# RGCN sums: one gathered chunk of every 64 fetched by SP, row by row

## What is computed

```python
seg  = concatenate([edge_type * n + src, (edge_type + R) * n + dst])
srcs = concatenate([dst, src])
for l in range(2):
    agg = segment_sum(output[srcs], seg, 2 * R * n).reshape(2 * R, n, -1)
    hidden = output @ W[-1] + b[-1]
    for r in range(R):
        for inv in (0, 1):
            s = r + R * inv
            msum = agg[s] @ W[s] + count[s] * b[s]
            hidden = 2.0 * (hidden + msum) / cnt[s]
    output = relu(hidden) if l == 0 else hidden
```

## Time and profile before

| | us |
|---|---|
| median of 3 runs | 4944.46 |
| lowest and highest | 4937.94, 4947.11 |
| time of the profiled execution | 4950.41 |
| its span | 4949.1 |

### The profile page before, as it was taken

One profiled execution on the slowest core, in us unless ns is written; L12 is line 12 of the kernel. 1 busy time (PEld: TensorE's weight loads), 2 busy tenths in 40 slices (PEclk: granted clock), 3 DMA queues, 4 the chain that ended last, 5 costly groups with the idle time before them and its releaser, 6 DMA issues. The chain is left out here.

```text
span 4949.1 us, 59313 instructions
## 1 busy us (share of the span) xinstructions
PE 3702.3 (75%) x16869; PEld 2389.1 (48%) x16871; DVE 2441.6 (49%) x3834; ACT 956.0 (19%) x2715; POOL 2069.4 (42%) x2229
## 2 busy tenths in 40 slices
PE   5977957798999989999898666676668444444459
PEld 2544523365555535555455555565555433333345
DVE  7989989216888841011327543444437422222221
ACT  2946848131000041111211000000001000000011
POOL 0000013104776501011012577777763777777740
PEclk7978979899999989999999765565559655555569
DMA  0000025717888726266264311111116211111114
GB/s 18 0 0 0 0 93 213 235 50 244 295 294 291 243 102 223 90 219 223 90 222 180 132 53 53 53 53 53 52 47 246 66 53 53 53 53 53 53 63 164
DMA packets 165366, 578.54 MB, mean 117 GB/s; under 512 B 47552, under 2 KB 59425, under 8 KB 164844
## 3 DMA queue, kind: packets, MB, share of 16 engines
q0 software_dynamic: 97200, 308.78, 19.4%
q1 hardware_dynamic: 67638, 267.41, 14.9%
q10 hardware_dynamic: 390, 0.60, 0.0%
HBM read 445.10 MB, written 131.53 MB: 117 GB/s over the span
## 5 line engine op out<-in xcount | busy, mean ns | idle before, releaser
L2126 PE MATMUL ps_sum_rgcn<-gathered_rgcn,select_sum_rgcn 128*128 x3328 | 987.0, 444 | 690.6 <-DMA gathered_rgcn<-by_dst,row 371.3
L2126 PEld LDWEIGHTS ps_sum_rgcn<-gathered_rgcn,select_sum_rgcn 128*128 128x128 f32 x3328 | 770.1, 311 | 766.9 <-issue 762.6
L2041 POOL DMA_INDIRECT gathered_rgcn<-by_dst,row x782 | 740.8, 947 | 238.3 <-issue 234.7
L2041 POOL DMA_INDIRECT gathered_rgcn<-by_src,row x686 | 647.3, 944 | 246.8 <-issue 202.4
L718 PE MATMUL ps_sum_arma<-gathered_sum_arma,select_sum_arma 128*128 128x384 f32 x1664 | 552.1, 491 | 20.7 <-DMA gathered_sum_arma<-arma,other 18.2
L704 POOL DMA_INDIRECT gathered_sum_arma<-arma,other x416 | 393.4, 946 | 378.2 <-POOLq L790 209.4
L1644 PE MATMUL ps_sum_arma<-pair_counts_sum_arma,parts_sum_arma 128*128 128x448 f16 x2625 | 520.6, 354 | 5.1 <-DMA pair_counts_sum_arma<-pairs 5.1
L2195 DVE TENSOR_TENSOR select_sum_rgcn<-one_hot_sum_rgcn,ps_coef_sum_rgcn 128x2048 f32<-128x2048 bf16 x52 | 119.0, 2288 | 680.3 <-PE ps_sum_rgcn L2126 680.2
L718 PEld LDWEIGHTS ps_sum_arma<-gathered_sum_arma,select_sum_arma 128*128 128x128 f32 x1664 | 308.8, 190 | 263.8 <-issue 60.3
L752 DVE TENSOR_TENSOR acc_arma_end<-acc_arma_end,ps_sum_arma 128x768 f32 x416 | 396.9, 954 | 57.8 <-PE ps_sum_arma L718 35.5
L2159 ACT COPY sums_or_hidden_rgcn<-ps_sum_rgcn 128x128 f32<-128x128 f32 x100 | 26.6, 266 | 1869.2 <-PE ps_sum_rgcn L2126 1869.2
(11 more groups left out here) (451 smaller groups left out, 5236.2 us busy)
## 6 DMA issues: line engine op xcount, KB each, us to landing
pair_counts_sum_arma<-pairs SPq DMA_DIRECT2D x125, 800.0 KB, 4.3
by_src<-rows_rgcn_src_table SPq DMA_DIRECT2D x50, 576.0 KB, 2.8
by_dst<-rows_rgcn_dst_table SPq DMA_DIRECT2D x50, 576.0 KB, 3.7
exact<-whole_pairs SPq DMA_DIRECT2D x25, 800.0 KB
pairs<-whole_pairs POOLq DMA_DIRECT2D x25, 800.0 KB, 5.8
pair_counts_sum_x<-pairs SPq DMA_DIRECT2D x25, 800.0 KB, 4.5
pair_counts_sum_gcn<-pairs SPq DMA_DIRECT2D x25, 800.0 KB, 4.5
air_counts_sum_neighbour<-pairs SPq DMA_DIRECT2D x25, 800.0 KB, 4.4
```

The costliest lines, as they stand in the source:

```text
L2041: nc.gpsimd.indirect_dma_start(got[:, n % PLACES, :], None, table, bass.IndirectOffsetOnAxis(ap=o.row[:, n % C:n % C + 1], axis=0)).then_i ...
L2126: nc.tensor.matmul(ps[:, bass.ds(slot, P)], select[:, parity, u, :], rows[:, bass.ds(place, D)], start=False, stop=False, skip_group_check ...
```

## The change

Five edits, all for the RGCN sums:

1. SP fetches the chunk of place 63 in 12 of the 13 turns: 128 transfers of one row of 512 bytes each, whose row number SP has loaded into a register (16 at a time, from a list `by_rows` on one partition). POOL leaves these chunks out.
2. Before the fetch of turn i SP waits until item 64i + 23 is done. PE waits for all 128 rows of turn i before item 64i + 60.
3. POOL's first 16 waits go by a list, `named`: for each group of four chunks the exact number of items up to its last chunk, in place of a number that allows for 24 second uses.
4. `EARLY` is 52 in place of 48.
5. The last additions to `acc` are made in 5 pieces of 5 tiles for each order.

To prepare 1 and 3, `sum_x` writes the row numbers to DRAM (two more loads, 768 numbers of 4 bytes each), `sum_gcn` reads them back on one partition, and `ring_lists` has 33 more instructions on DVE.

```diff
-EARLY = 3 * U
+EARLY = 3 * U + GROUP
+NAMED = 16
 SHARED = NT - 1

+def by_rows(n):
+
+    return n % PLACES == PLACES - 1 and fetched(n)
...
 def ring_lists(nc, k, tile_of, place_of, then):
+
+    chunk_of = tile_of[:, 0, :]
+    for g in range(NAMED):
+        upto = float(g * GROUP + GROUP - 1)
+        then(nc.vector.tensor_scalar(chunk_of, k.orders[0].chunk_of[:, :], upto, None, ALU.is_le))
+        then(nc.vector.tensor_reduce(k.named_f[:, g:g + 1], chunk_of, AX.X, ALU.add))
+    then(nc.vector.tensor_scalar(k.named[:, :], k.named_f[:, :], float(U), None, ALU.add))
...
+        def fetch_rows(sp):
+
+            def chunk(i, table):
+
+                for p in range(0, P, U):
+                    at = nc.values_load_multi_w_load_instructions(
+                        k.by_rows[0:1, bass.ds(i * P + p, U)], engines=(mybir.EngineType.SP,), min_val=0,
+                        max_val=NP * R - 1, skip_runtime_bounds_check_because="rows of the tables")[1]
+                    for u in range(U):
+                        sp.dma_start(got[p + u:p + u + 1, PLACES - 1, :], table[bass.ds(at[u], 1), :]).then_inc(rows_landed, 16)
+
+            first_of_next = len([t for t in ROW_TURNS if t * PLACES + PLACES - 1 < C])
+            chunk(0, tables[0])
+            for start, end, table in ((1, first_of_next, tables[0]), (first_of_next, len(ROW_TURNS), tables[1])):
+                with sp.Fori(start, end) as i:
+                    sp.wait_ge(multiplied, i * PLACES + SHARED + U)
+                    chunk(i, table)
...
             for n in range(EARLY, TOTAL * U):
-                if not fetched(n):
+                if not fetched(n) or by_rows(n):
                     continue
+                if n == PLACES:
+                    named = nc.values_load_multi_w_load_instructions(
+                        k.named[0:1, 0:NAMED], engines=(mybir.EngineType.Pool,), min_val=U, max_val=C + U,
+                        skip_runtime_bounds_check_because="counts of items")[1]
                 if n % Q == 0 and n >= PLACES:
-                    gp.wait_ge(multiplied, n + Q - PLACES + SHARED + U)
+                    g = (n - PLACES) // GROUP
+                    gp.wait_ge(multiplied, named[g] if g < NAMED else n + Q - PLACES + SHARED + U)
...
                     g = (at * U + u) // GROUP
+                    if g == GROUPS - 1 and (skipped is not None or i in ROW_TURNS):
+                        pe.wait_ge(rows_landed, (i + 1) * (16 * P))
...
             for n in range(ORDERS):
-                if n:
-                    dve.wait_ge(added, n)
-                dve.wait_ge(taken, n * NT + NT)
-                nc.vector.tensor_tensor(acc[:, :, :], acc[:, :, :], sums[:, n, :, :], ALU.add).then_inc(added, 1)
+                for g in range(TURNS):
+                    here = slice(g * J, g * J + J)
+                    dve.wait_ge(taken, n * NT + g * J + J)
+                    if n:
+                        dve.wait_ge(added, g + 1)
+                    nc.vector.tensor_tensor(acc[:, here, :], acc[:, here, :], sums[:, n, here, :], ALU.add).then_inc(added, 1)
```

More of the change, by code:

```diff
@@ L1960, in fetched, with of_turn @@
     return n % C < CHUNKS
+def by_rows(n):
+    return n % PLACES == PLACES - 1 and fetched(n)
 def due(group, turn):
-    return sum(fetched(t * PLACES + group * GROUP + m) for t in range(turn + 1) for m in range(GROUP))
-def ring_lists(nc, k, tile_of, place_of, then):
+    chunks = [t * PLACES + group * GROUP + m for t in range(turn + 1) for m in range(GROUP)]
+    return sum(fetched(n) and not by_rows(n) for n in chunks)
+def of_turn(group):
+    return sum(not by_rows(group * GROUP + m) for m in range(GROUP))
+ROW_TURNS = [t for t in range(2 * C // PLACES) if by_rows(t * PLACES + PLACES - 1)]
+def ring_lists(nc, k, tile_of, place_of, then):
+    chunk_of = tile_of[:, 0, :]
[4 more added lines that the diff above has]
+    then(nc.vector.tensor_scalar(k.named[:, :], k.named_f[:, :], float(U), None, ALU.add))
     for n, o in enumerate(k.orders):
@@ L2018, in typed_sum_stage, with _ @@
         block = c.block()
[L2020 to L2024, removed]
+        (rows_landed,) = c.sems("rows_landed")
+        def fetch_rows(sp):
[12 more added lines that the diff above has]
+                    chunk(i, table)
+        @block.sync
+        def _(sp):
+            for to, source in loads:
+                sp.dma_start(to, source).then_inc(loaded, 16)
+            fetch_rows(sp)
+            if loads:
                 sp.wait_ge(loaded, 16 * len(loads))
+            sp.wait_ge(rows_landed, 16 * P * len(ROW_TURNS))
         def after(i, at, steps):
@@ L2117, in step @@
                     g = (at * U + u) // GROUP
+                    if g == GROUPS - 1 and (skipped is not None or i in ROW_TURNS):
+                        pe.wait_ge(rows_landed, (i + 1) * (16 * P))
                     if skipped is not None:
[L2119 removed]
+                        pe.wait_ge(arrived[g], ((i + 1) * of_turn(g) - skipped[g] + before[g]) * 16)
                     elif due(g, i) > due(g, i - 1):
@@ L2138, in _ @@
             for start, end in ((0, HALFWAY), (HALFWAY + 1, TURNS_OF_STEPS - 1)):
-                skipped = [start * GROUP - due(g, start - 1) for g in range(GROUPS)]
+                skipped = [start * of_turn(g) - due(g, start - 1) for g in range(GROUPS)]
                 with pe.Fori(start, end) as i:
@@ L2269, in scaled, with dram_rows @@
     return finish
+def dram_rows(k, dram, n):
+    mine = [i for i, t in enumerate(ROW_TURNS) if (t * PLACES + PLACES - 1) // C == n]
+    first = (ROW_TURNS[mine[0]] * PLACES + PLACES - 1) % C
+    chosen = k.orders[n].row[:, 0:len(mine) * PLACES].rearrange("p (c a) -> p c a", a=PLACES)[:, :, first]
+    return dram["by_rows"].rearrange("(c p) o -> p (c o)", p=P)[:, mine[0]:mine[-1] + 1], chosen
 def arma1_layer(nc, k, A, dram, xcur):
@@ L2284, in arma1_layer @@
             (dram["loop"].rearrange("(t p) o -> p (t o)", p=P), k.dinv_loop[:, :]),
+            *(dram_rows(k, dram, n) for n in (0, 1)),
             (k.gcn_w[:, :], A["L1_gnn_W"]), (k.gcn_bias[:, :], A["L1_gnn_b"].rearrange("(p o) -> p o", o=1))]
@@ L2430, in gcn_layer @@
         loads += typed_loads(k, A, 0)
+        loads += [(k.by_rows[:, :], dram["by_rows"].rearrange("n o -> o n"))]
         loads += [
@@ L2542, in gnn_kernel @@
                 ("arma1", NP, K * HID, F32), ("by_src", NP, R * D, F32), ("by_dst", NP, R * D, F32),
-                ("exact", NP, NP, U16), ("rows", NP, PARTS * P, BF16), ("pairs", NP, NP, FP16), ("loop", NP, 1, F32))}
+                ("exact", NP, NP, U16), ("rows", NP, PARTS * P, BF16), ("pairs", NP, NP, FP16), ("loop", NP, 1, F32), ("by_rows", len(ROW_TURNS) * P, 1, I32))}
     with ExitStack() as c:
@@ L2560, in gnn_kernel @@
             k.look_at = late.sb("look_at", [P, 2 * C], I32)
+            k.by_rows = late.sb("by_rows", [1, len(ROW_TURNS) * P], I32)
+            k.named = late.sb("items_of_first_chunks", [P, NAMED], I32)
+            k.named_f = late.sb("items_of_first_chunks_f", [P, NAMED])
             k.typed_w = late.sb("typed_w", [P, S2 + 1, D])
```

2 lines of the change are left out of this document (added).

## The result

The changed kernel takes 5177.61 us (median of 4 runs, 5174.18 to 5178.99), the kernel before 4945.78 beside it: ratio 1.0466, 95% interval 1.0452 to 1.0481. It is slower by 232 us, where 589 was forecast. The direction and the place were right; the sum was two and a half times too large.

The account below looks back on a forecast made before the run. POOL's gathers were taken to bound the sums before, SP's row fetches after: 372 (layer 0) + 213 (layer 1) - 5.6 + 6 + 4 = 589 us slower, about 5533 us; forecast 5300 to 5700, range 5130 to 5830.

Parts of the forecast that it names:

- The price of one row on SP: SP's fetch of one row: address 55, MOVE 29, issue 332, gaps 120 ns, together 536 ns, 68.6 us for 128 rows.
- T: Time one chunk occupies SP, rows plus register loads: 77.7 us, bounds 75 to 100.
- An issue well under 0.3 us: Sign that would show the prediction wrong, on SP's row transfers, expected at about 332 ns an issue.
- the second rival: "Cheaper, but not enough": an SP issue of 0.2 us, T 60.8, about 5130 us; chance 0.09.
- The window: RGCN sums: SP's fetch must fit 36 items, 44.9 us, but needs 79.9; turns 108.5 us (layer 0, +372), 93.9 (layer 1, +213).
- break-even: Layer 1 of the RGCN sums: POOL stays the bound there if T is at most 62.4 us.
- The other edits: Last additions -5.6 us, named waits and early gathers 0, `sum_gcn` list work +6, `sum_x` small numbers +4.
- the first rival: "SP is cheap and the change pays": POOL stays the bound in the sums, 4895 us; chance 0.16.
- SP is cheap and the change pays: POOL stays the bound: layer 0 -35, layer 1 -19, total -49, 4895 us; issue at most about 0.10 us; chance 0.16.
- Cheaper, but not enough: SP issue of 0.2 us, T 60.8: layer 0 still loses, layer 1 nearly holds, 5130 us; chance 0.09.
- SP's issues queue behind one another: Issue of 427 ns, row 631 ns, T 89.9, total 5826 us; chance of 5700 or more 0.15.

Follow-up runs that it names:

- shapes: Kernel before plus 64 SP transfers beside each sum stage, eight back to back of each of several shapes, to an unread tile: 4944.83 us beside 4951.65.
- after_2: The changed kernel run once more, on a chip where the kernel before takes 4945.77 us: 5170.6 us, ratio 1.0457.
- rows_164: Changed kernel with 36 more one-row transfers in each of SP's lists, into a tile that nobody reads: 5445.08 us, ratio 1.1003.
- no_rows_2: Kernel before with only the named waits, 52 early gathers and divided additions; POOL gathers every chunk: 4931.92 us, ratio 0.9965.
- two_rows_2: Changed kernel with 64 transfers of two neighbouring rows a list instead of 128 of one (second row not the wanted one): 4903.73 us, ratio 0.9917.
- spare_place_late_list: spare_place_2 with the two small stores of row numbers moved from sum_x's loads to behind those of sum_arma1: 4910.52 us, ratio 0.9931.
- spare_place_2: Changed kernel with one more ring place for every second turn's rows, so SP may start a turn earlier; lists written out: 4910.09 us, ratio 0.9928.
- rows_aside_2: Changed kernel with SP's rows sent to a tile that nobody reads, while POOL gathers every chunk: 4937.61 us, ratio 0.9988.
- no_rows: Same kernel as no_rows_2, on the slower chip where the kernel before took 5407.17 us: 5393.1 us, ratio 0.9974.

## Why the size was wrong

**The price of one row on SP: the step that failed.** "The issue hardly knows size" was true of the loads and table stores that the prediction had the earlier trace rows, since 16 engines share each of them (16 packets of 4 bytes each in the trace of before). It took 332 ns as "the row nearest in kind", by the address, with 320 as the lower bound. What counts is how many engines share the transfer, as `shapes` shows, and not the register: one row goes through one engine. The last store of 53 rows was a one-engine transfer too, but its 365 ns were those of an issue right behind another; the second 53-row transfer in `shapes` took 367, the first 230. Measured a row: 37 + 29 + 225 and 117 ns of gaps, 0.408 us, for 55 + 29 + 332 + 120 = 536. The gaps were right, the fused operation 18 ns too dear, the issue 107. The register load was nearly right (1.141 for 1.10), some 10 us a list for 9.1. So T is 62.3 from first issue to last and 63.6 with the first register load, not 77.7, and outside the bounds of 75 to 100 that the text gave. An issue well under 0.3 us stood in the prediction as a sign of being wrong. The total of 5178 still lies in its range of 5130 to 5830, which was wide enough to hold the second rival, but outside the 5300 to 5700 of its own forecast.

The Trainium skill's page "DMA: Bandwidth & Descriptors" (section "Why a DMA increments its semaphore by 16 and not by 1") has a figure for previous generations, 512 sequencer cycles, from which the prediction estimated 427 ns for an issue. The 225 ns of a one-row issue here disagree with it further than the 332 of the trace before did; only transfers shared by 16 engines and sent back to back come near it, with 420 and 432 ns in `shapes`.

**The window: right.** From item 23 of a turn to PE's start at item 60 it took 65.1 us (0.1 to the register load, 63.6 of list, 1.3 to 1.4 of landing), where T = 62.4 and the forecast landing of 2.2 give 64.6. With T = 62.4 the prediction's own formula gives turns of 62.4 + 2.2 + 28.6 = 93.2 us in layer 0 and 62.4 + 2.2 + 14.0 = 78.6 in layer 1. Measured: 92.6 and 78.7. Its sum then is +201 for layer 0 (item 60 at PE's own 2835, 11 x 93.2, the 54 us behind), +29 for layer 1, and with the other terms -5.6, +6 and +4 it is +234. Measured +232, or +225 in `after_2`. That it is so close is in part luck: in the first profile layer 0 lost 13 us less than the +201 (4.5 less up to item 60, 6 in the turns, 2.5 behind them), and the stages ahead of the sums lost about 5 more than forecast. All but some 2 us of the gap to 589 is T: 15.3 us by 24 is 367, less the 12.8 that can't be had in layer 0's first turn, where PE's own pace takes over. `rows_164` shows the slope by itself, 23.2.

**Layer 1 at its break-even.** The prediction put it at T = 62.4, and T is that. PE waits 40 to 47 us a turn for SP (29 in the first), and the turn is as long as POOL's 63 gathers (78.6): PE waits in one piece for SP where it waited in many for POOL. The +27.5 is a balance. Up to item 124 PE waits for SP's first two lists and takes 136.3 us for 94.6: +42. In the middle of the layer, where one table ends and some chunks aren't fetched, the turn took 48.8 us before (item 380 to item 444); SP's chain knows no such rest, and it now takes 77.6: +29. The last 68 items lie in store and take 31.4 us for 64.3: -33. The nine turns between take 1.1 less each: -10.

**The other edits.** In this execution `sum_x` and `sum_gcn` cost more than the 10 forecast:

```profile
921.31 7.79 SPq L1602 DMA_DIRECT2D pair_counts_sum_x<-pairs  x1
929.14 0.44 SPq L1605 DMA_DIRECT2D by_rows<-row  x1
929.62 2.65 SPq L1602 DMA_DIRECT2D pair_counts_sum_x<-pairs  x1
932.31 0.44 SPq L1605 DMA_DIRECT2D by_rows<-row  x1
```

```profile
940.90 5.49 PE L1644 MATMUL ps_sum_x<-pair_counts_sum_x,parts_sum_x 128*128 128x448 f16 x21 [7.70 <-DMA pair_counts_sum_x<-pairs]
949.45 5.82 PE L1644 MATMUL ps_sum_x<-pair_counts_sum_x,parts_sum_x 128*128 128x448 f16 x21 [3.05 <-DMA pair_counts_sum_x<-pairs]
957.70 2.79 PE L1644 MATMUL ps_sum_x<-pair_counts_sum_x,parts_sum_x 128*128 128x448 f16 x7 [2.43 <-DMA pair_counts_sum_x<-pairs]
```

These are SP's queue and PE's waits in `sum_x`: one wait of 4.69 us has become three with 13.2 together, 8.5 more for a forecast of 4. The drain of `sum_gcn` starts 12.0 us later, 5.9 of which the stage had brought with it; that leaves 6.1, for 6: DVE's list work ends at 2611.49, and the drain that had 9.64 us of slack starts at once. But between executions the start of layer 0 moves: over the kernels that carry these edits it lay between 1 us earlier and 18 us later than before. A term of this size can be read from one profile only as "some 10 us". The named waits and early gathers were put at 0, and that holds while SP is the bound; with POOL as the bound they are worth 13 us net (`no_rows_2`), of 25.1 won in the layers (now 923.2 and 917.6 us), where the first rival had 21 + 5.

**The rivals.** "SP is cheap and the change pays" needed T of at most 51; `two_rows_2` is that case, with T near 37, and it took 4904 where the rival said 4895. "Cheaper, but not enough" was the truth: it assumed an issue of 0.2 us and T = 60.8, and gave 5130. It had a chance of 0.09 because the lower bound for an unseen shape was set by shapes that were seen. "SP's issues queue behind one another" was wrong here; it describes transfers shared by 16 engines (316 ns for the first and 420 behind one another, 357 and 432 in `shapes`), not one row.

That 24 gathers less on POOL pay once nobody waits for SP is shown by `spare_place_late_list` against `no_rows_2`, of one set: 4911 and 4932, 21 us for 24 x 1.248 = 30, less what the rest of the change costs. `spare_place_2` beats both kernels, by 0.7% of before; on the slower chip the same kernel lost 11%. `no_rows_2` wins 0.35% and was no slower than before on either. Which of them to take depends on which chips it must run on.

## What to carry to other kernels

When a transfer moves to another queue, write down when that queue may start and how much work is left behind the consumer's wait; that window, times the number of turns, decides, and here its slope was right (24 us a us forecast, 23 measured) while the price of one instruction was not. If the sum has such a slope, the price it multiplies has to be known for the very shape of the transfer, so keep the range open below the nearest rows when these all have another shape; how many DMA engines share it belongs to the shape. A second place, which lets the queue start a turn earlier, here turned the same loss into the same gain as a list of half the length.

## What the runs showed of the hardware

- SP's issue of a transfer went by the number of DMA engines that shared it. In medians, back to back: 225 to 252 ns for one row of 512 bytes (1 engine), 237 to 253 for 2 rows (2), 295 for 4 (4), 420 for 16 (16) and 381 to 432 for 128 (16).
- Issues of 53 rows, all through one engine, took 230 ns for the first, 358 to 367 for the next two, and then 1.2 to 1.9 us each, about the pace at which that engine moved them (1.4 us each). With 16 and 128 rows, on 16 engines, nothing of the kind was seen.
- 3072 one-row transfers beside POOL's gathers cost them nothing measurable (`rows_aside_2`: layers within 1.5 us of `no_rows_2`), on a chip where the kernel before took 4946.
- On one chip the kernel before took 5407 us instead of 4946. There the pauses between POOL's gathers, 0.30 us as a rule, were now and then longer without any PE wait, as here in `no_rows`, and SP's instructions, 29 ns as a rule for a MOVE, stretched to 1.4 us and more beside them:

```profile
3316.45 0.94 POOL L2056 DMA_INDIRECT gathered_rgcn<-by_src,row  x1 [0.30 <-issue]
3320.04 0.94 POOL L2056 DMA_INDIRECT gathered_rgcn<-by_src,row  x1 [2.64 <-DMA gcn_bias<-in_L_gnn_b]
```

The releaser that the view names there is a small load issued many stages earlier, so it isn't the cause; the cause stays open.
